# Turning x's one-byte codes on TensorE as 32-bit words of four

## The reference

```python
def fake_quant(x, scale, zp):
    s = scale.reshape(()); z = zp.reshape(())
    q = jnp.clip(jnp.round(x / s + z), QMIN, QMAX)      # 0 .. 255
    return (q - z) * s
...
x = x + matmul(fake_quant(layernorm(x), s1, z1), fake_quant(ctx, s2, z2))
x = x + ffn(layernorm(x), gate_w, gate_b, w1, b1, w2, b2)
```

## Time and profile before

| | us |
|---|---|
| median of 3 runs | 399.52 |
| lowest, highest | 399.23, 400.81 |
| the profiled execution's own time | 398.93 |
| its span in the profile | 397.1 |

### The profile page before, as it was taken

The page is one execution under the profiler, slowest core; times in us unless marked ns, Lnnn a source line. Parts: engine busy times, 40 slices in busy tenths (PEclk is TensorE's granted clock), DMA queues, the critical chain, the costliest instruction groups (busy, mean ns, idle before and its releaser), DMA issues.

```text
span 397.1 us, 5246 instructions
## 1 busy us (share of the span) xinstructions
PE 382.7 (96%) x1860; PEld 302.4 (76%) x1860; DVE 319.9 (81%) x529; ACT 194.9 (49%) x253; POOL 75.6 (19%) x94
## 2 busy tenths in 40 slices
PE   1999989999999999999999999999999999999996
PEld 1445736888888888888888888888888888888885
DVE  8799959999499899898899995654997864629972
ACT  3578655174347635471854832345475244434720
POOL 8648400442300001063203001030000010110000
PEclk9999999999999999999999999999999999999999
DMA  8997039538745586628003888864065784550112
GB/s 306 414 408 303 3 103 378 210 117 201 134 80 165 206 250 221 166 53 156 4 0 111 302 282 293 232 126 87 0 225 166 249 285 83 106 106 2 54 53 107
DMA packets 27437, 66.98 MB, mean 169 GB/s; under 512 B 2160, under 2 KB 2192, under 8 KB 27280
## 3 DMA queue, kind: packets, MB, share of 16 engines
q1 hardware_dynamic: 23888, 54.01, 38.6%
q0 software_dynamic: 3456, 12.58, 16.6%
q10 hardware_dynamic: 64, 0.02, 0.0%
HBM read 49.83 MB, written 4.19 MB: 136 GB/s over the span
## 4 chain that ended last, share of the span: by engine, by line
PE 88%; DVE 5%; DMA 2%; issue 1%; ACT 1%; SPq 1%; POOL 1%; POOLq 0%; ACTq 0%; DVEq 0%
PE ps L1655 44%; PE ps L1623 38%; PE ps L1415 3%; DMA raw<-in_ctx_dram 2%; DVE xres L911 2%; DVE bn L840 1%; PE ps L1449 1%; PE ps L1403 1%; DVE hT_lo L920 0%; DVE q L874 0%; SPq L318 0%; SPq L323 0%; POOL ctxq L453 0%; DVE q_bias L1147 0%; PE ps L1484 0%
## 5 line engine op out<-in xcount | busy, mean ns | idle before, releaser
L1037 DVE TENSOR_TENSOR w_lo<-raw,w_hi 128x1024 fp32r<-128x1024 f32 x88 | 103.3, 1216 | 0.9 <-ACT w_hi L688 0.6
L688 ACT ACTIVATE w_hi<-raw 128x1024 fp32r<-128x1024 f32 x88 | 87.8, 1051 | 30.9 <-DVE raw L1050 18.0
L1655 PE MATMUL ps<-hT_hi,w_hi 128*128 128x512 f32 x256 | 99.9, 390 | 0.0
L1655 PE MATMUL ps<-hT_lo,w_hi 128*128 128x512 f32 x256 | 99.6, 389 | 0.0
L1655 PE MATMUL ps<-hT_hi,w_lo 128*128 128x512 f32 x256 | 99.6, 389 | 0.0
L1623 PE MATMUL ps<-w_hi,a_hi 128*128 128x512 f32 x224 | 87.4, 390 | 0.0
L1623 PE MATMUL ps<-w_hi,a_lo 128*128 128x512 f32 x224 | 87.2, 389 | 0.0
L1623 PE MATMUL ps<-w_lo,a_hi 128*128 128x512 f32 x224 | 87.1, 389 | 0.0
L776 ACT ACTIVATE act_f<-ps,b1T 128x512 f32<-128x512 f32 x32 | 22.1, 690 | 115.7 <-PE ps L1655 115.7
L523 POOL DMA_DIRECT2D raw<-raw x24 | 21.3, 1040 | 194.4 <-DMA raw<-in_L_ffn_w_dram 140.1
L1655 PEld LDWEIGHTS ps<-hT_hi,w_hi 128*128 128x128 f32 x256 | 48.1, 188 | 10.2 <-issue 0.2
(11 more groups left out here) (155 smaller groups left out, 368.6 us busy)
## 6 DMA issues: line engine op xcount, KB each, us to landing
raw<-in_L_ffn_w_dram SPq DMA_DIRECT2D x64, 512.0 KB, 5.1
raw<-raw POOLq DMA_DIRECT2D x24, 512.0 KB, 6.6
raw<-in_ctx_dram SPq DMA_DIRECT2D x16, 512.0 KB, 11.5
xres<-in_x_dram SPq DMA_DIRECT2D x8, 512.0 KB, 9.6
out_dram<-xres SPq DMA_DIRECT2D x16, 256.0 KB, 4.1
b2row<-in_L_ffn_b_dram SPq DMA_DIRECT2D x4, 512.0 KB, 5.8
gate_rows<-in_L_ffn_gate_w_dram SPq DMA_DIRECT2D x1, 1536.0 KB, 18.7
small<-in_L_xattn_x_scale_dram ACTq DMA_DIRECT2D x2, 0.0 KB
```

Of the source, the lines that this page charges most:

```text
L688: nc.scalar.activation(w_hi[n % SLOTS][:, 2 * c:2 * c + 2, :], region(q)[:, 2 * c:2 * c + 2, :], ACT.Copy).then_inc(w_hi_ready, 1)
L1037: V.tensor_tensor(w_lo[n % SLOTS][:, 2 * c:2 * c + 2, :], region(n % QUARTERS)[:, 2 * c:2 * c + 2, :], w_hi[n % SLOTS][:, 2 * c:2 * c + 2, ...
L1655: last = T.matmul(ps[:, G1_BANK + f % 2, :], w[q % SLOTS][:, k % TT, fs], h[:, k, :], start=n == 0, stop=n == 3 * KT - 1)
```

## The change

The codes of `x` are kept as plain bytes: `q1` becomes two slots of 1024 bytes, seen by TensorE as 256 fp32 words of four codes each. A tile is turned in two fp32 pieces of 128x128 words and not in eight fp16 ones; after this a PSUM word in partition `p` of piece `h` holds the four codes of columns `512h + 4p + j`, `j` from 0 to 3. `load_q1T` picks the bytes apart: it reads PSUM as one-byte elements four bytes apart, through an access pattern with one dimension more, and subtracts the zero point alone. The columns that stand in one `q1T[:, k, :]` are now those with `k = 4h + j`, so the context's tile `k` is loaded with rows `512h + 4p + j`: every fourth row, still 128 rows of 4 KB, of a block of 512. The memset of `q1` and the waits for it go away. `off1` loses the 1024.

```diff
-FILL_ORDER = {"dve": [0, 1, 2],
+FILL_ORDER = {"dve": [1, 2],
...
+WORDS = D // 4
...
-    ctx_v = ctx_in.rearrange("b (k p) n -> (b k) p n", p=P)
+    ctx_v = ctx_in.rearrange("b (h p j) n -> b h j p n", h=2, j=4)
...
-        q1 = sb("q1", [P, 2, D], F16, o); o += 2 * D * 2
-        q1c = q1[:].bitcast(U8).rearrange("p k (n two) -> p k n two", two=2)[:, :, :, 0]
+        q1 = sb("q1", [P, 2, WORDS], F32, o); o += 2 * D
+        q1c = q1[:].bitcast(U8)
...
+        def packed_codes(i):
+
+            words = ps[:, Q1T_BANK[i], 0:WORDS]
+            return words.bitcast(U8).rearrange("p (h s j) -> p h j s", h=2, j=4)
...
-                sp.dma_start(raw[:, c % RAW, :], ctx_v[c]).then_inc(raw_in[c % RAW], 16)
+                sp.dma_start(raw[:, c % RAW, :], ctx_v[c // KT, c % KT // 4, c % 4]).then_inc(raw_in[c % RAW], 16)
...
             def quant_x(i):
...
                 dve.wait_ge(q1_scale_ready, i + 1)
-                wait_fill(dve, 0)
...
-                V.tensor_scalar(q1T[i // TT][:, :, i % TT * P:(i % TT + 1) * P],
-                                ps[:, Q1T_BANK[i], :].bitcast(F16).rearrange("p (k s) -> p k s", k=KT),
+                V.tensor_scalar(q1T[i // TT][:, :, i % TT * P:(i % TT + 1) * P].rearrange("p (h j) s -> p h j s", j=4),
+                                packed_codes(i),
                                 off1, None, ALU.add).then_inc(q1T_ready["dve"], 1)
...
-                V.tensor_scalar(off1, mid1, -1.0, -OFF, ALU.mult, ALU.add).then_inc(off1_ready, 1)
+                V.tensor_scalar(off1, mid1, -1.0, None, ALU.mult).then_inc(off1_ready, 1)
...
-            fill(0)
             fill(1)
...
-                bank = ps[:, Q1T_BANK[i], :].bitcast(F16)
-                for k in range(KT):
-                    last = T.transpose(bank[:, k * P:(k + 1) * P], q1[:, i % 2, k * P:(k + 1) * P], ident_b[:])
+                for h in range(2):
+                    last = T.transpose(ps[:, Q1T_BANK[i], h * P:(h + 1) * P],
+                                       q1[:, i % 2, h * P:(h + 1) * P], ident[:])
                 last.then_inc(q1T_ps, 1)
```

More of the change, by code:

```diff
@@ L443, in fill @@
             def fill(n):
-                dst = q1[:, :, :] if n == 0 else ctxq[(n - 1) // 4][:, (n - 1) % 4 * 2:(n - 1) % 4 * 2 + 2, :]
+                dst = ctxq[(n - 1) // 4][:, (n - 1) % 4 * 2:(n - 1) % 4 * 2 + 2, :]
                 G.memset(dst.bitcast(F32), FILL).then_inc(fill_done["pool"], 1)
@@ L458, in quant_x @@
                 pool.wait_ge(q1_scale_ready, i + 1)
-                wait_fill(pool, 0)
                 if i >= 2:
@@ L571, in quant_x @@
                 act.wait_ge(q1_scale_ready, i + 1)
-                wait_fill(act, 0)
                 if i >= 2:
@@ L617, in load_q1T @@
                 act.wait_ge(off1_ready, 1)
-                nc.scalar.activation(q1T[i // TT][:, :, i % TT * P:(i % TT + 1) * P],
-                                     ps[:, Q1T_BANK[i], :].bitcast(F16).rearrange("p (k s) -> p k s", k=KT),
+                nc.scalar.activation(q1T[i // TT][:, :, i % TT * P:(i % TT + 1) * P].rearrange("p (h j) s -> p h j s", j=4),
+                                     packed_codes(i),
                                      ACT.Identity, bias=off1).then_inc(q1T_ready["act"], 1)
```

## The result

The changed kernel takes **402.22 us** (median of 6 executions, 401.51 to 403.45), the kernel before 399.56 in the same comparison: ratio 1.0064, 95% interval 1.005 to 1.0078. It is slower by 2.7 us; the forecast was 399.9, no measurable change. The profiled execution has a span of 401.7 and a time of 403.45.

A forecast was written before the change was run, and what follows sets the result against it. TensorE's experts' products bound it from 63.30 us, behind a chain over DMA, POOL, TensorE and DVE. +0.03 + 0.3 = +0.33 on 398.93 gives 399.26; the median stands 0.59 above, so 399.9 us, range 398.6 to 401.6.

The forecast's parts named there:

- The loads' price: Loads out of PSUM reading bytes: DVE 1.22 us, 0.48 more for each of two loads; ACT unchanged at 1106 ns.
- POOL behind `split_row_term`: At about 24.1 us DVE's `split_row_term` starts first and holds POOL's power step of tiles 4 and 5: +0.3 us.
- each saving only lengthens an idle time: TensorE's savings behind tiles 4 and 5, 6 and 7 (0.45, 0.22, 0.22 us) fall into waits, so gain nothing.
- The pitch: The context's DMAs go from 4 to 16 KB pitch in HBM, same 4 KB rows and queue: 0 in the forecast.
- The rival: The pitch slows the context's DMAs, delaying context tile 11 past 30.53 us: 401.8 at 360 GB/s; chance 0.06.
- The credit of 0.45 us: Turning tiles 2 and 3 is on the path and gets 0.45 us shorter, so `load_q1T(3)` starts at 19.48, not 19.93.
- Tile 3's load, followed on: Step on DVE's load of tile 3: starts earlier, takes longer, ends at 20.70 against 20.68, +0.03 us for later statistics.
- The rival on TensorE's clock: Fewer pieces of tiles 0 and 1 delay TensorE's rise from 1.2 GHz, slowing first matmuls: +0.9, so 400.8; chance 0.12.
- What was to cost nothing: Removed memset and waits, `quant_x` byte writes (within 0.2), `off1`, and the context's DMAs at the new pitch: 0.
- The idle times of the earlier trace: TensorE's waits behind tiles 4 to 7 (0.70, 0.40, 0.21 us) stay open; their closing would prove the reasons wrong.

## Why the prediction was wrong

**The loads' price** held: 1.22 us was the estimate for DVE, 1.28 the row; 1.1 for ACT, 1.10 the row. The Trainium skill ("VectorE: DVE Perf Modes", section "Mode 2×_1P — pack two bf16 into one 32-bit read") asks for 16-bit elements at step one for two results per cycle. The traces agree: 1278 ns for bytes, 741 for fp16. Whether the type or the step costs was not tested apart.

**POOL behind `split_row_term`** held: +0.3 was the term, 1.01 for 0.72 the row, in the changed kernel and with byte loads alone. By the Trainium skill ("SBUF — State Buffer", section "Who interferes with whom") a DVE instruction with two SBUF inputs contends with a GpSimd one that reads SBUF. The traces agree: the step takes 0.72 where it starts ahead of `split_row_term` and 1.01 where it starts behind it.

**The step that failed** first is "each saving only lengthens an idle time", a price of nothing for TensorE's savings behind tiles 4 to 7. The runs show about 1.0 us in its place: with short transposes the granted clock fell in 30 of 49 executions, and filling the idle times with constants took the falls and 1.0 us away (401.66 for 402.67). The reason that was given, the idle time, was not the right one either. The 1.49 us at 37 us (0.70 before) come with the byte loads alone, fp16 pieces and all, and none of the 20 executions of the two kernels of that kind has a fall. What the short transposes add by themselves is smaller: 0.63 for 0.40 us ahead of the product with `ones` at 52.8 us, and 0.41 for 0.21 ahead of the gate's logits at 54.8.

**The pitch**, put at 0, is the second term that failed; it measured 0.5. The rival had it at context tile 11, where there was no loss: the DMA ran at 407 to 412 GB/s from 20 to 32 us. The dip stood at 8 to 9 us, in front of context tile 0, in all thirteen profiles with the new rows (223 to 339 GB/s) and in none of the six with the old (400 GB/s or more). It moved tile 0's codes from about 10.3 to 11.1. That the dip is the pitch's doing, and not that of another property of the order, was not tested apart.

**The credit of 0.45 us** in "Tile 3's load, followed on" is the third. The pair of tiles does take 0.45 for 0.89, and the load starts 0.64 behind the pair and not 1.09. But the forecast held the pair's own start fixed, and it lies anywhere from 18.8 to 21.8 us in the nineteen profiles: it hangs on when the first context tile has landed and on how many of the products ahead run at the lower level, four to fourteen. No run shows the credit in the time. With no fall in either kernel, short transposes with filled idle times took 401.66 against 401.19 for the long ones, 0.5 more where the credit makes it less; the two means are not sharp enough (0.7 either way) to exclude it. Without the credit the prediction's sum is +0.8, so 400.3: still inside its range. It was the two terms put at nothing that took the time out of it.

**The rival on TensorE's clock** (chance 0.12) named a thing that did happen. In the changed kernel the first product at 0.38 us starts at 17.8 us, for 13.6 before, and twelve products are slow for four. But not the pieces alone decide it: in the old row order it starts between 13.6 and 15.7 with long transposes and at 14.7 and 15.1 with short ones, while in the new order it starts between 17.1 and 19.2 in nine of thirteen profiles, two of them with all the fp16 pieces. The other four are one of the kernel before with the new rows (14.6) and the three with constants near tiles 0 and 1 (15.2 to 16.1). So a part of what the new rows cost may be this late rise; these are single profiles, and its price was not measured apart. What the rival didn't ask is what the clock does later.

**The gap of 0.27 us** between two statistics, 0.36 from one row to the next, was foreseen by nothing.

**What was to cost nothing** shows no cost where it was looked at: the fill and ACT's loads. The idle times of the earlier trace rows didn't close. The range, 398.6 to 401.6, left out the truth because the small terms all lay on the same side: +0.9, +0.5 and +1.5, and none was in the sum at its size.

## What to carry to other kernels

A saving on an engine that waits anyway is not always worth nothing; it can cost. When work is taken off TensorE, compare the granted clock of many executions before and after, and read it stretch by stretch in several profiles, since one profile shows a fall or shows none. The idle times alone didn't tell which kernel would fall. A packed format moves its price to who unpacks it: cost the reading engine first. Here ACT read bytes at no extra charge and DVE did not. Take no credit for an earlier step until you have named what its start hangs on.

## What the runs showed of the hardware

- At the start the products run at 0.58 to 0.63 us each while the granted clock reads 1.00 (in the run with early constants in the kernel before it reads 0.50 there). The first one at 0.38 starts at 13.6 us before and at 17.8 after, and between 14.6 and 19.2 in the other runs. The rows are the changed kernel's:

```profile
L1417 PE MATMUL ps<-ctxq,q1T x5: 630/634/634, 14.4 to 16.1; 128*128 128x512 f16 x5
L1417 PE MATMUL ps<-ctxq,q1T x6: 379/564/634, 16.1 to 18.0; 128*128 128x512 f16 x6
```

- Falls of the clock to 0.50 stood at 37 to 42 us in the two profiles of the changed kernel and between 52 and 60 in six others with short transposes; they lasted 3 to 7 us. One more stood at 8 to 15 us, with early constants and the fp16 pieces. A long idle time alone doesn't bring one: with constants ahead of every tile TensorE was busy for 0.52 of 2.00 us at 36 to 38 as well, and the clock stayed. What decides is open.
- The gap of 0.27 to 0.28 us between `x_stats(4)` and `x_stats(5)` stands in all eight profiles in which DVE's list is the changed kernel's, and in none with one more or one fewer instruction ahead of it or another order. Its cause is open.
- Bytes written four apart cost 1526 ns on ACT for 1232, 1484 on DVE for 1244 and 1491 on POOL for 1195; bytes read four apart from PSUM cost ACT nothing (1101 ns for 1106).
